# Relational graph layers on one core: the third layer's node table given up, its ratio gathered per edge

## The reference, cut to what matters

```python
x = _layernorm(x + gcn(x, edge_index, W1, b1, W2, b2))      # two convolutions
x = _layernorm(x + mean_by_relation(x, W[8], root, bias))   # x @ root + bias, plus a mean per relation
x = _layernorm(x + attention(x, W[8]))                      # scores per edge, softmax per relation
x = _layernorm(x + relu(sum_by_relation(x, W[16])))         # out = segment_sum((x @ W[type])[src], dst)
```

## Time and profile before

| | us |
|---|---|
| median of 3 runs | 4078.74 (4078.26 to 4087.64) |
| span of the profiled execution | 3581.7 |
| median less span | 497.0 |

### The profile page before, as it was taken

How to read it: one execution, slowest core, us unless ns; L and a number is a source line. 1 busy time by engine, 2 the same in 40 slices (tenths; PEclk the granted TensorE clock), 3 DMA queues, 4 the chain that set the end, 5 groups by cost and what they waited for, 6 DMA issues and landing times. The chain is left out here.

```text
span 3581.7 us, 56712 instructions
## 1 busy us (share of the span) xinstructions
PE 2802.1 (78%) x10941; PEld 1590.5 (44%) x10941; DVE 2825.5 (79%) x8091; ACT 1733.7 (48%) x4763; POOL 1671.5 (47%) x1582
## 2 busy tenths in 40 slices
PE   2676641777556667999979999778889799999997
PEld 1444431666455553444434454433333344444443
DVE  7997661888688886999956666678888688888886
ACT  1776771999555553455445555445555311111111
POOL 2777776555444434554435555300000256666664
PEclk9998885999888887999989999989999899999998
DMA  2666551555444442333346666534444311111111
GB/s 66 215 216 185 176 167 38 173 176 172 129 155 147 145 142 77 93 89 91 92 139 212 214 217 215 171 100 137 140 132 146 102 38 48 48 49 50 50 51 34
DMA packets 275110, 450.96 MB, mean 126 GB/s; under 512 B 53226, under 2 KB 121353, under 8 KB 275034
## 3 DMA queue, kind: packets, MB, share of 16 engines
q1 hardware_dynamic: 224858, 363.81, 32.4%
q0 software_dynamic: 50176, 86.35, 8.9%
HBM read 247.71 MB, written 206.12 MB: 127 GB/s over the span
## 5 line engine op out<-in xcount | busy, mean ns | idle before, releaser
L1218 PE MATMUL bank<-sum_masked,sum_w 128*128 128x512 f32 x1568 | 691.4, 594 | 1.4 <-DVE sum_masked L1308 1.4
L1103 POOL DMA_INDIRECT sum_rows<-t_x,m_row_int x196 | 223.6, 1141 | 751.2 <-POOLq L112 536.8
L1308 DVE SCALAR_TENSOR_TENSOR sum_masked<-sum_typ,sum_col 128x512 f32<-128x512 bf16 x784 | 488.7, 684 | 19.7 <-ACT sum_col L1148 17.5
L1218 PEld LDWEIGHTS bank<-sum_masked,sum_w 128*128 128x128 f32 x1568 | 291.4, 191 | 332.4 <-issue 268.3
L1549 PE MATMUL bank<-at_masked,at_ww 128*128 128x512 f32 x784 | 365.6, 610 | 42.0 <-DVE at_masked L1598 42.0
L1218 PE MATMUL bank<-mean_masked,mean_w 128*128 128x512 f32 x784 | 380.7, 614 | 18.8 <-DVE mean_masked L1308 18.8
L1218 PE MATMUL bank<-att_masked,att_w 128*128 128x512 f32 x784 | 379.8, 614 | 11.6 <-DVE att_masked L1308 10.7
L1598 DVE SCALAR_TENSOR_TENSOR at_masked<-at_typ,at_col 128x512 f32<-128x512 bf16 x392 | 243.7, 684 | 168.8 <-ACT at_col L1525 165.9
L1490 POOL DMA_INDIRECT at_rows<-t_x,m_row_int x196 | 253.1, 1291 | 261.7 <-DMA source_rows<-at_rows 169.6
L1103 POOL DMA_INDIRECT mean_rows<-t_x,m_row_int x196 | 208.3, 1063 | 244.8 <-ACT mean_scaled L1136 152.4
L1148 ACT ACTIVATE sum_col<-bank 128x512 f32<-128x512 f32 x49 | 29.3, 597 | 578.6 <-PE bank L1264 565.0
(11 more groups left out here) (282 smaller groups left out, 5675.8 us busy)
## 6 DMA issues: line engine op xcount, KB each, us to landing
pf_xc<-x_dram SPq DMA_DIRECT2D x98, 256.0 KB, 3.0
t_g<-pf_g SPq DMA_DIRECT2D x98, 256.0 KB
t_x<-pf_x SPq DMA_DIRECT2D x98, 256.0 KB
c_dense_x<-t_x SPq DMA_DIRECT2D x98, 256.0 KB, 3.4
t_x<-c_dense_x SPq DMA_DIRECT2D x98, 256.0 KB, 3.3
at_late_x<-t_x SPq DMA_DIRECT2D x49, 512.0 KB, 4.0
t_x<-at_late_x SPq DMA_DIRECT2D x49, 512.0 KB, 4.7
c_same<-p_same SPq DMA_DIRECT2D x98, 128.0 KB, 3.4
```

The costliest lines, as they stand in the source:

```text
L1103: pool.indirect_dma_start(rows[:, s % 2, j, :], None, source, bass.IndirectOffsetOnAxis(ap=index[:, k:k + 1], axis=0))\
L1218: pe.matmul(H[q][:, :], w[:, r, :], masked[:, r % MASKS, :], start=(r == 0), stop=(r == n_rel - 1))\
L1308: v.scalar_tensor_tensor(out=masked[:, r % MASKS, :], in0=typ[:, q, :], scalar=float(r), in1=col[:, q, :], op0=ALU.is_equal, op1=ALU.mult) ...
```

## The change

Table X3 is gone. The weighted stage writes its slots into X2, beside X2's node rows, and the last stage gathers from X2. A gathered slot row is a row of layer three already; a gathered node row is one of layer two and has to be multiplied by ratio 0. So the last stage scales every gathered row by a factor per edge, `source_col`: 1 where `row_int` points to a slot, the source node's ratio where it points to a node row. The ratios reach the edges through DRAM: `m.ratio` now has the two ratios of a node side by side, SP stores it to `ratio_table` at the start of the mean stage (401 KB, ahead of the first relation types), POOL gathers a pair of numbers per edge into `m.info` at the start of the weighted stage (196 gathers), and DVE makes `source_col` of them at the start of the last stage (four operations of 128 x 196).

The late rows are now all in the score stage: eight rows per batch and partition times ratio 1, stored to the output (512 KB). The weighted stage has none.

```diff
     def shifts(self, v, s, q):
         if runs(s):
             v.wait_ge(self.scale_ready, s + 1)
-            ratio = self.m.ratio[:, :, bass.ds((s * 2 + self.parity) * BT, BT)]
+            ratio = self.m.ratio[:, bass.ds((s * 2 + self.parity) * BT, BT), :].rearrange("p r l -> p l r")
...
                 last = act.activation(self.x[i][:, q, j, :], self.x2[:, q, j, :], ACT.Copy,
-                                      scale=self.m.ratio[:, layer, bass.ds(s * 2 * BT + self.first + j, 1)])
+                                      scale=self.m.ratio[:, bass.ds(s * 2 * BT + self.first + j, 1), layer])
...
-                sp.dma_start(self.rows(self.m.tables[("X3", "OUT")[layer]], s, chunks * BT), self.x[i][:, q])\
+                sp.dma_start(self.rows(self.m.tables["OUT"], s, chunks * BT), self.x[i][:, q])\
...
-        factor = {CONV1: m.norm_col, MEAN: m.weight_col, ATTEND: m.alpha_col}.get(kind)
+        factor = {CONV1: m.norm_col, MEAN: m.weight_col, ATTEND: m.alpha_col, SUM: m.source_col}.get(kind)
...
-        if kind == ATTEND:
-            late = LateRows(m, sb, sem, 1, 1, [(1, 1)])
...
+            if kind == MEAN:
+                sp.dma_start(m.ratio_table.rearrange("(p r) l -> p (r l)", p=P),
+                             m.ratio[:, :, :].rearrange("p r l -> p (r l)")).then_inc(ratio_stored, 16)
...
-                if kind == ATTEND:
-                    late.load(sp, b + 2, q)
-                    late.store(sp, b - 1, 1 - q)
...
+            if kind == MEAN:
+                hold(sp, ratio_stored, 16)
...
         @block.gpsimd
         def _(pool):
+            if kind == ATTEND:
+                for k in range(KT):
+                    pool.indirect_dma_start(m.info[:, k, :], None, m.ratio_table,
+                                            bass.IndirectOffsetOnAxis(ap=m.src_int[:, k:k + 1], axis=0))\
+                        .then_inc(gathered[0], 16)
+                hold(pool, gathered[0], KT * 16)
...
+            if kind == SUM:
+                act.wait_ge(factor_ready, 1)
...
-                if kind == ATTEND:
-                    late.scale(act, b, q, 0)
...
+            if kind == SUM:
+                v.tensor_scalar(has_edges[:, :], m.row_int[:, :], float(NP), None, ALU.is_ge)
+                v.tensor_scalar(own_rows[:, :], m.row_int[:, :], float(NP), None, ALU.is_lt).then_inc(factor_step, 1)
+                v.wait_ge(factor_step, 1)
+                v.tensor_tensor(own_rows[:, :], own_rows[:, :], m.info[:, :, 0], ALU.mult).then_inc(factor_step, 1)
+                v.wait_ge(factor_step, 2)
+                v.tensor_tensor(m.source_col[:, :], own_rows[:, :], has_edges[:, :], ALU.add).then_inc(factor_ready, 1)
...
-        late = LateRows(m, sb, sem, 0, 2, [(0, 2), (1, 1)])
+        late = LateRows(m, sb, sem, 0, 2, [(1, 2)])
...
-                late.scale(act, b, q, 1)
...
-        edge_stage(nc, io, m, ATTEND, None, m.tables["X3"], io["W_att"], R8)
-        edge_stage(nc, io, m, SUM, m.tables["X3"], m.tables["OUT"], io["W_sum"], R16)
+        edge_stage(nc, io, m, ATTEND, None, m.tables["X2"], io["W_att"], R8)
+        edge_stage(nc, io, m, SUM, m.tables["X2"], m.tables["OUT"], io["W_sum"], R16)
```

More of the change, by code:

```diff
@@ L1018, in edge_stage @@
         w_loaded = sem("w_loaded")
+        if kind == MEAN:
+            ratio_stored = sem("ratio_stored")
+        if kind == SUM:
+            factor_step, factor_ready = sem("factor_step"), sem("factor_ready")
+            own_rows, has_edges = sb("own_rows", [P, KT]), sb("has_edges", [P, KT])
         gathered = sem.of_pool("gathered")
@@ L1087, in _ @@
                 dense.all_stored(sp)
-            if kind == ATTEND:
-                late.all_stored(sp)
+            if kind == MEAN:
+                hold(sp, ratio_stored, 16)
             if kind != SUM:
@@ L1714, in build @@
     m.tables = {"G1": dram("t_g1", (NP + EP, D)), "X1": dram("t_x1", (NP + EP, D)),
-                "X2": dram("t_x2", (NP + EP, D)),
-                "X3": dram("t_x3", (NP + EP, D)), "OUT": io["out"]}
+                "X2": dram("t_x2", (NP + EP, D)), "OUT": io["out"]}
     m.info_table = dram("t_info", (NP, 2))
+    m.ratio_table = dram("t_ratio", (NP, 2))
     m.same_plane = dram("p_same", (EP,), BF16)
@@ L1734, in build @@
         m.dstraw_col, m.hi_col, m.lo_col, m.score_col = map(column, ("dstraw", "hi", "lo", "score"))
-        m.norm_col = column("norm")
+        m.norm_col, m.source_col = column("norm"), column("source")
         m.weight_col, m.alpha_col, m.ends_col = map(column, ("weight", "alpha", "ends"))
-        m.node, m.ratio = sb("node", [P, RPP]), sb("ratio", [P, 2, RPP])
+        m.node, m.ratio = sb("node", [P, RPP]), sb("ratio", [P, RPP, 2])
         m.dst_int, m.hi_int, m.lo_int, m.src_int, m.last_int, m.row_int = (
```

## The result

| | us |
|---|---|
| kernel before, median of 4 runs | 4083.19 (4078.26 to 4091.54) |
| changed kernel, median of 4 runs | 4264.30 (4260.54 to 4268.09) |
| ratio, with its 95% interval | 1.0454 (1.0435 to 1.0473) |
| predicted | 4014 (3955 to 4066) |

A forecast was written before the change was run, and what follows sets the result against it. The score stage was taken as bound by a loop through ACT's wait for the late store, the last stage by PE. Terms -61 - 6 + 1.5 + 0.5 = -65 us from the 4078.7 us median gave 4014 us, range 3955 to 4066.

The forecast's parts named there:

- 497.0 us lie around the span, and I keep them as they are: Whole kernel: median 4078.7 us less profiled span 3581.7 us, taken as unchanged time outside the span.
- I price the disturbance at 0 to 1 us for the 27 batches: Weighted stage: cost of 196 ratio-pair gathers on POOL to its row loads, 0 to 1 us over the 27 batches they last.
- Rival (d): Weighted stage: 8-byte gathers crowd the row loads, landing in 5.8 instead of 3.6 us, +59 us, time 4079; chance 0.04.
- "-6" for the late traffic: Weighted stage: net change of -6 us, from a range of -36 to +27, for late traffic removed and gathers added.
- the bound of 36: Weighted stage: gain of at most 36 us, if every row load landed in 3.1 us.
- I take 4.6: Score stage: assumed landing of the late rows' store, 4.6 us, giving 8.5 us a batch and a 61 us gain.
- my upper end: Score stage: longest landing allowed for the late store, 6.2 us, with five transfers issued in one row.
- Rival (b): Score stage: store and source rows land later, 6.2 to 7.1 us, gain 1 to 23, time about 4065; chance 0.13.
- the 8.5 predicted: Score stage: pace of 8.5 us a batch from DVE's two-batch loop, against 9.77 before.
- +1.5: Last stage: four added scales a batch lie within ACT's wait for PE; only the first batch is exposed, +1.5 us.
- +0.5: Mean stage: the 401 KB ratio store stands on SP ahead of the first types, 0 to 1.5 us, taken as +0.5.

## Why the prediction was wrong, point by point

- **"497.0 us lie around the span, and I keep them as they are": the first failed step.** 1.7 us lie around it. Some 420 of the 497 us are prefill time beside rows of gathers and 76 lie in the first convolution, in every profiled execution but the first. The sum itself doesn't use the 497, since it goes by differences; the harm is that rows of this one execution were taken for those of the timed ones. A gap of 12% between a profile and its median was work that the profile didn't show, and the text gave it no mechanism.
- **Weighted stage, "I price the disturbance at 0 to 1 us for the 27 batches": the step that decided.** The row of gathers cost 220 us in all (645.8 against 426.0 without it; 219 when added to the kernel before). The price came from the earlier trace rows, loads that land in 3.0 us beside such a row, and these are from the one execution without the disturbance. Rival (d) named the right place with a chance of 0.04, but by another mechanism, row loads that land late (+59): ACT waited 2.8 us for them between 2860 and 3085, and 207.9 for its column copy.
- **Weighted stage, "-6" for the late traffic: too small.** Without the gathers the masks took 426.0 instead of 454.6, so 29 us, inside the bound of 36; the stage reaches the mean stage's pace. Whether it was the late traffic behind the row loads or the four late scales on ACT is not taken apart.
- **Score stage, "I take 4.6": mis-sized.** The masks went from 476.1 to 467.4, 9 us instead of 61. The structure was right (the store's landing closes the loop, 9.4 by the sum and 9.61 measured), but the landing measured 5.6 and 7.3 us, where 6.2 was my upper end. Rival (b) had it: 6.2 to 7.1, a gain of 1 to 23. The sum had the load ahead of the store, but priced what the load costs the store's landing at 1.6 us at most and then took hardly any of it; with the store first it lands in 3.1. That the pace then came to 8.66, near the 8.5 predicted, is luck: the landing that it was worked out from, 4.6, is not the one that either order shows.
- **Last stage, "+1.5": right in kind.** 712.9 against 713.7 us of masks, and from the weighted stage's last mask to the first of this one 27.4 us against 26.4. ACT's wait for PE is 479.0 / 41 = 11.7 us a batch before and 430.9 / 41 = 10.5 now, so the four scales lie in it as said; the kernel before, then the changed one:

```profile
ACT sum_col L1148 <- PE bank L1264: 479.0, 41, 11.8
```

```profile
ACT sum_col L1160 <- PE bank L1274: 430.9, 41, 10.6
```

- **Mean stage, "+0.5": right.** Its masks took 422 to 432 us over the runs of both kernels, a spread above the term. But from ACT's last `c_new` of the second convolution to the stage's first mask it is 19.7 to 20.0 us in the traces of the old kernel and its variants, and 20.3 to 20.9 in those of the changed one, so some 0.7 us.
- **The range** failed by its premise: its ends bounded the terms of the sum by rows of one execution, and nothing in it stood for that execution not being the timed one.

## What to carry to other kernels

Let gathers by index go in short rows of four to eight with a wait in between, on their own landing if on nothing else: in the weighted stage that wait left 1 to 14 us of the unbroken row's 220. Put a store that is waited for ahead of a load that isn't, when both share a queue. And when a profile's span and the median differ by more than a few us, profile again before pricing anything by its rows.

## What the runs showed of the hardware that was not expected

- An unbroken row of 196 gathers by index (1.28 us apart) slowed PE, DVE and ACT from a batch in 9 us to one in some 67, with the DMA engines at 14 GB/s. Gathers of 32 rows did it as much as of 128, rows of 8 bytes (weighted stage) as rows of 512 (prefill); plain transfers and fills did not.
- The slow part sets in about 10 us after the row's start and lasts about 20 us beyond its end; against the stage without gathers (426.0), rows of 8 cost 14 us in all, rows of 16 168 and the whole row 220.
- Left open: why the execution of the first profile ran the prefill's rows without loss, at 1.33 to 1.35 us a gather instead of 1.27 to 1.29, and its first convolution 76 us faster; what it is that fills up; and how much of the paced prefill's 6.6 us a chunk, where 4.7 was seen, comes from its rows of 8 to 24. Every timed run listed with the experiments also has a span (1.7 us below its time), so each was recorded as it ran, and none shows whether the recording has a part in the loss.
